# Two small memsets on GpSimd behind each row scatter of a routed mixture-of-experts kernel

## The reference

```
x = x + 0.5 * ffn(layernorm(x))        # expert pass 1
x = x + attention(layernorm(x))        # differential attention, two softmaxes, RMS norm
x = x + 0.5 * ffn(layernorm(x))        # expert pass 2, same weights

def ffn(t):
    logits = t @ Wr.T + br              # 8 experts
    top_v, top_i = top_k(logits, 2)     # two experts for each row
    w = softmax(top_v)
    h = relu(t @ W1[e].T + b1[e]); o = h @ W2[e].T + b2[e]
    return layer_norm(t + sum of w * o over the row's two experts) * gamma + beta
```

## Time and profile before

| | |
|---|---|
| median of three runs | 677.21 us |
| span of the profiled execution, first to last instruction | 746.1 us |
| mean granted TensorE clock in it | 0.908 of full |
| TensorE busy | 595.6 us (80%) |
| VectorE busy | 454.9 us (61%) |
| ScalarE busy | 443.2 us (59%) |
| GpSimd busy | 380.9 us (51%) |
| row scatters, line 465 | 128 DMAs, 100.1 + 30.6 us on GpSimd |
| sends, line 489 | 78 DMAs, 79.2 us on GpSimd |

### The profile page before, as it was taken

One profiled execution on the slowest core, in us unless ns is written; L12 is line 12 of the kernel. 1 busy time (PEld: TensorE's weight loads), 2 busy tenths in 40 slices (PEclk: granted clock), 3 DMA queues, 4 the chain that ended last, 5 costly groups with the idle time before them and its releaser, 6 DMA issues.

```text
span 746.1 us, 16949 instructions
## 1 busy us (share of the span) xinstructions
PE 595.6 (80%) x4276; PEld 544.6 (73%) x4276; DVE 454.9 (61%) x1432; ACT 443.2 (59%) x1144; POOL 380.9 (51%) x475
## 2 busy tenths in 40 slices
PE   2626189999999879899898998969288479999955
PEld 1625079999998768787886897858187479999821
DVE  5527445654667788799688789655035236457636
ACT  4434056666665677678786866837054236786744
POOL 6345225541445277568324575835745645545633
PEclk9965579999999999999999999989679679999969
DMA  8412124443333111010000000212221222522042
GB/s 278 141 38 65 50 60 102 110 104 84 98 98 90 51 29 29 8 30 22 1 1 1 23 30 15 69 29 63 57 58 54 69 74 54 175 64 59 28 147 84
DMA packets 54253, 49.22 MB, mean 66 GB/s; under 512 B 9926, under 2 KB 45938, under 8 KB 53904
## 3 DMA queue, kind: packets, MB, share of 16 engines
q1 hardware_dynamic: 45312, 31.25, 15.0%
q0 software_dynamic: 8640, 16.87, 7.3%
q10 hardware_dynamic: 208, 0.02, 0.0%
HBM read 25.99 MB, written 23.02 MB: 66 GB/s over the span
## 4 chain that ended last, share of the span: by engine, by line
PE 51%; DVE 19%; issue 9%; another core or an unknown queue 7%; POOL 6%; ACT 6%; DMA 1%; ACTq 1%; DVEq 0%; POOLq 0%; SPq 0%
PE banks L953 17%; PE banks L963 16%; DVE nb L1607 4%; PE banks L946 3%; PE banks L1050 3%; DVE scratch L1614 2%; PE banks L885 2%; PE banks L887 2%; PE banks L886 2%; POOL zb L478 1%; POOL rs L455 1%; ACT scratch L639 1%; POOL rows L465 1%; DVE st_r L1217 1%
## 5 line engine op out<-in xcount | busy, mean ns | idle before, releaser
L963 PE MATMUL banks<-blocks,scratch 128*128 x1248 | 172.8, 283 | 24.6 <-issue 21.9
L963 PEld LDWEIGHTS banks<-blocks,scratch 128*128 128x128 f32 x1248 | 158.3, 199 | 26.8 <-issue 26.7
L953 PE MATMUL banks<-scratch 128*128 128x128 f32 x1248 | 173.4, 284 | 4.3 <-ACT scratch L639 3.0
L1357 DVE TENSOR_SCALAR scratch<-banks,blocks 128x128 f32<-128x128 f32 x312 | 95.2, 347 | 120.5 <-PE banks L953 68.8
L953 PEld LDWEIGHTS banks<-scratch 128*128 128x128 f32 x1248 | 157.9, 198 | 9.4 <-issue 9.2
L465 POOL DMA_INDIRECT rows<-rowbuf,slot x96 | 100.1, 1043 | 55.6 <-issue 48.6
L633 ACT ACTIVATE scratch<-banks 128x128 f32<-128x128 f32 x156 | 43.3, 277 | 136.0 <-PE banks L946 66.5
L489 POOL DMA_INDIRECT results<-scratch x78 | 79.2, 1015 | 77.0 <-DVE scratch L1365 45.4
L646 ACT ACTIVATE scratch<-banks,blocks 128x128 f32<-128x128 f32 x312 | 96.8, 366 | 14.3 <-remote 6.6
L721 ACT ACTIVATE scratch<-banks,nb 128x1024 f32<-128x1024 f32 x64 | 71.3, 1115 | 45.7 <-DVE nb L1607 45.1
L639 ACT ACTIVATE scratch<-blocks 128x512 f32 x156 | 97.5, 625 | 0.0
(11 more groups left out here) (210 smaller groups left out, 882.7 us busy)
## 6 DMA issues: line engine op xcount, KB each, us to landing
scratch<-rows SPq DMA_DIRECT2D x156, 64.5 KB
yrows<-scratch SPq DMA_DIRECT2D x78, 64.0 KB
rows<-padrows SPq DMA_DIRECT2D x34, 64.5 KB
x<-in_L_attn_x_dram SPq DMA_DIRECT2D x4, 512.0 KB, 5.6
scratch<-in_L_ffn_W_dram SPq DMA_DIRECT2D x1, 2048.0 KB, 19.3
rows<-rowbuf,slot POOLq DMA_INDIRECT x96
results<-scratch POOLq DMA_INDIRECT x78
zb<-results SPq DMA_DIRECT2D x1, 1024.0 KB
```

Of the source, the lines that this page charges most:

```text
L953: ins = pe.matmul(hT_at(T, c), staged(T, c), xT_of(T), start=True, stop=True)
L963: ins = pe.matmul(y_at(T), hT_of(T, c), blocks[:, W2_AT + c * D:][:, bass.ds(at, D)], start=(c == 0), stop=(c == FC - 1))
L1357: ins = dve.tensor_scalar(hT_of(T, c), hT_at(T, c), blocks[:, B1_AT + c:][:, bass.ds(at, 1)], 0.0, ALU.add, ALU.max)
```

## The change

A tile `idle` of 128 x 8 is added. `rest()` clears it twice with GpSimd memsets, each waited for. A rest stands behind each of the 32 row scatters of the prologue, before and behind each of the 10 row scatters of batch 2 that follow sends in pass 2, and before, between and behind the two row scatters of batch 3 at each of the tiles 16 to 23. The row scatters of pass 1 and of the attention stay as they are.

```diff
+        idle = sb("idle", 8)
...
             for b in range(BATCHES):
                 rstd(b)
+            def rest():
+
+                for _ in range(2):
+                    steps.then(pool.memset(idle[:, :], 0.0))
+
             for b in range(GB):
-                scatter(0, b)
+                for i in range(PAIRS):
+                    scatter(0, b, range(i, i + 1))
+                    rest()
             for s in range(SLOTS):
...
             for s in range(SLOTS):
                 send(s)
                 if s < PAIRS - 6:
+                    rest()
                     scatter(1, BATCHES - 2, range(s + 6, s + 7))
+                    rest()
                 if ROWS_AT <= s < ROWS_AT + TB:
                     i = 2 * (s - ROWS_AT)
-                    scatter(1, BATCHES - 1, range(i, i + 2))
+                    for k in range(2):
+                        rest()
+                        scatter(1, BATCHES - 1, range(i + k, i + k + 1))
+                    rest()
```

## The result

The change makes the kernel slower: 708.41 us against 677.68, a ratio of 1.046 (interval 1.0436 to 1.0478). I had forecast 694.5 with a range to 707: the direction was right, the time 13.9 us too low, and the range too short.

What follows compares the result with a forecast made beforehand. GpSimd's DMA queue was taken to bound pass 2 and, tied with VectorE's path, the prologue. Rests add 5.7 in the prologue and 11.6 in pass 2, 17.3 in sum: 677.2 + 17.3 = 694.5 us, range 671 to 707.

Steps and rivals of the forecast that it cites:

- the unnamed waits: Waits without a named releaser in prologue and pass 2, 21.3 and 52.9 us, said to belong to the profiled execution.
- My sum of 685.9: Profiled span less the unnamed waits, 671.9, plus 14.0 by which GpSimd's queue is late in pass 2.
- each DMA is 0.17 cheaper in timed runs: GpSimd's DMAs in timed runs cost some 8.7 / 50 = 0.17 us less each than in the profile.
- a slack of 5.4: Prologue: 32 x 0.17 us by which the scatters' path could be ahead of VectorE's path, both tying at 75.0.
- 5.7 for the prologue: Cost of 31 rests before the prologue's last scatter: the middle between 3.0 and 8.4 us.
- GpSimd's queue bounds pass 2: Issuing 50 sends and row scatters takes 64.0 us, making tile 39 of pass 2 14.0 late.
- 0.27 for a rest: Two waited memsets between GpSimd DMAs stretch the spacing from 1.26 to 1.53 us; bounds 0.17 and 0.44.
- 43 x 0.27 = 11.6: Pass 2: 43 rests before the last row scatter, all 11.6 us counting because the queue is bound.
- My upper bound: A rest costs up to 0.44 us, since 5 of 30 DMAs behind compute take 2.06 to 2.09.
- a rest breaks the run and pays: First rival: unnamed waits are in timed runs too, and rests in prologue and pass 2 remove them; 672, chance 0.25.
- it is hidden: Second rival: rests cost nothing, prologue bound by VectorE's path and pass 2's queue not bound; 677, chance 0.09.
- The third rival: Compute after a DMA is dearer than its row, or late loads lower TensorE's clock; 700 to 710, chance 0.12.

Runs made afterwards that it cites:

- e5: The kernel before, unchanged, profiled a second time: the profiled execution took 680.1 us, with a span of 678.3.
- e1: The kernel before with only the 32 rests of the prologue, none in pass 2: 687.67 us, 9.3 over before.
- e8: The kernel before, no rests, with 7 instead of 3 row scatters of batch 2 ahead of GpSimd's statistics wait in pass 2: 671.40 us against 678.91.
- e6: The whole change, but each memset clears its own 8 columns and GpSimd waits for none: 679.12 us against 678.91 of before.
- e4: The kernel before with 26 rests in pass 2 alone, only ahead of row scatters, none ahead of a send: 685.25 us, 6.9 over before.
- e9: As e4, but the row scatters of batches 2 and 3 in pass 2 carry a bounds check: 698.51 us beside 677.67 of before.
- e3: The kernel before with 18 rests in pass 2 alone, each just ahead of a send: 694.38 us, 16.1 over before.
- e10: The kernel before, no rests, with a bounds check on the row scatters of batches 2 and 3 in pass 2: 678.13 us beside 677.67.

## Why the prediction was off

- **That the unnamed waits aren't in the timed runs**: right. e5 has none. I had 75.0 for the first transpose without them; it is 74.4. But I had set them all beside long runs of scatters, and that reading was wrong: the first expert pass has some too (VectorE's 3.13 at 186.5), and took 156.4 against 151.0. My sum of 685.9 was a span, and e5's span is 678.3: of the 7.6 between them 5.4 sat in that pass, 1.8 in pass 2 (89.1 against 87.3) and 0.6 in the prologue.
- **That each DMA is 0.17 cheaper in timed runs**: wrong. This was invented to explain the 8.7 between my sum and the median. The sum was a span and the median a time, and in every run here the time is 1.7 to 1.8 more than the span, so even the 8.7 was 10.5. In e5 a scatter comes every 1.26 us, as in the earlier trace rows. It gave the scatters of the prologue a slack of 5.4 against VectorE's path. In e5 they have none: the first transpose, at 74.38, waits for the loaded rows, and VectorE's last operation before it had ended at 73.6. I put 5.7 for the prologue; e1 measured 9.3 and the traces 9.1, so this term was 3.4 too small.
- **That GpSimd's queue bounds pass 2**: right. 87.3 for 39 tiles that need 75 at TensorE's pace, and e8's gain. Of the lateness I had 14.0; it is 12.3 by e5 (87.3 less 75.0).
- **0.27 for a rest**: right ahead of a row scatter (0.26), by luck in its parts. The DMA behind it takes 0.97, not 1.06, and the idle time is 0.28, not 0.16.
- **The step that failed: 0.27 for every rest in pass 2, "43 x 0.27 = 11.6".** 17 of the rests stand ahead of a send that counts, and its idle time behind them is 0.90. With 17 x 0.62 = 10.5 and the 1.1 of the two long row scatters more the term is 22.8 (at 0.26 the 43 rests are 11.2), and the traces show 22.5. The miss of 10.9 here and of 3.4 in the prologue are the whole of it. The row that I took the 0.16 from was a DMA behind a compute instruction that it doesn't wait for; a rest ends in a wait. My upper bound was built from rare long DMAs of over 2 us, none of which came in the two places, and not from what a wait in front of a DMA can uncover.
- **Rivals**: that a rest breaks the run and pays, no; that it is hidden, no for waited memsets and yes for unwaited ones (e6). By the Trainium skill ("DMA: Bandwidth & Descriptors", section "Anatomy of one DMA — SWDGE (gpsimd) path") descriptor generation is a small part of a DMA's fixed time. By that the sum would have been near 0, and e1's 9.3 for 31 rests of 0.26 speaks against it here. The "42 us of plain issue" that I set against this rival are 40.4 by the earlier trace rows (20.2 twice). The third rival had the time (700 to 710) but not the cause: the memsets cost what their row says, and it is the start of the DMA behind them that is dearer. TensorE's clock in the stretch fell from 0.99 to 0.92 only, and what comes behind the stretch took as long as in e5 (116.6 to the end against 116.3).

## What to carry to other kernels

A profile that is 69 us longer than the timed runs has to be taken again before its waits are explained; here none of its unnamed waits came again in twelve later profiles. On an engine that issues DMAs, ask what stands between the last wait and the DMA: here the idle time before it was covered only where another DMA, with nothing waiting for it, stood in between. And where a queue is the bound, look for its idle time first: moving four DMAs into a gap gained 7.5 us by the medians, 4.8 of them seen in the traces, where no spacing gained anything.

## What the hardware showed that I had not expected

- Behind a wait on its own engine an indirect DMA of GpSimd started 0.28 us later (after, e4), 0.80 with a bounds check (e9), 0.85 without a check but with separate waits and a counter in between (after, e1), 0.90 with both (after, e3); behind a DMA all of them started 0.30 later (e5, e10).
- Behind a 0.20 us operation that nothing waits for it started 0.18 later, and 0.53 with the check (e4, e10).
- Two unwaited memsets of 128 x 8 between two such DMAs cost about 0.02 us a pair (e6); waited for, 0.26 (after).
- Two profiled executions of the same instructions had spans of 746.1 and 678.3 (before, e5).
